# Second attention: exponentials mixed in single precision as the moving operand, values in 32-column groups

## The reference, cut to what matters

```python
    def _L1_attn_ref(hidden_states, W_attn, b_attn, P_q, P_k, P_v, W_back, W_proj, b_proj):
        B, S, D, DC, H = (4, 512, 192, 96, 12)
        HD = DC // H
        b, s, _ = hidden_states.shape
        qkv = hidden_states @ W_attn + b_attn
        q, k, v = jnp.split(qkv, 3, axis=-1)
        q = q @ P_q
        k = k @ P_k
        v = v @ P_v
        split = lambda t: t.reshape(b, s, H, HD).transpose(0, 2, 1, 3)
        qh, kh, vh = (split(q), split(k), split(v))
        scores = jnp.einsum('bhqd,bhkd->bhqk', qh, kh) / jnp.sqrt(jnp.float32(HD))
        causal = jnp.tril(jnp.ones((s, s), dtype=scores.dtype))
        scores = scores * causal + -10000.0 * (1.0 - causal)
        weights = jax.nn.softmax(scores, axis=-1)
        ctx = jnp.einsum('bhqk,bhkd->bhqd', weights, vh)
        ctx = ctx.transpose(0, 2, 1, 3).reshape(b, s, DC)
        out = ctx @ W_back
        out = out @ W_proj + b_proj
        return out
```

## Time and profile before

| | |
|---|---|
| median of the runs | 991.69 us |
| the runs | 990.14, 994.79, 991.69 us |
| profiled execution, from first to last instruction | 992.2 us |
| granted TensorE clock, mean of the span | 0.787 |
| TensorE matmuls busy | 726.5 us (73%) |
| VectorE busy | 696.7 us (70%) |
| ScalarE busy | 672.9 us (68%) |
| GpSimd busy | 345.5 us (35%) |

### The profile page before, as it was taken

How to read it: one execution, slowest core, us unless ns; L and a number is a source line. 1 busy time by engine, 2 the same in 40 slices (tenths; PEclk the granted TensorE clock), 3 DMA queues, 4 the chain that set the end, 5 groups by cost and what they waited for, 6 DMA issues and landing times. The chain is left out here.

```text
span 992.2 us, 19112 instructions
## 1 busy us (share of the span) xinstructions
PE 726.5 (73%) x7022; PEld 534.0 (54%) x7023; DVE 696.7 (70%) x1406; ACT 672.9 (68%) x1236; POOL 345.5 (35%) x265
## 2 busy tenths in 40 slices
PE   2693661452696748999997488867775898999985
PEld 1562330221475424599997444324444467999984
DVE  3588989999598888654453476986988874554543
ACT  1578947999697858755554279568993761767664
POOL 6720920000000000468775424680000202577763
PEclk9786555555698757999999789555557899999999
DMA  6446770000221319534333466370002952243332
GB/s 190 137 84 190 210 219 10 8 17 0 72 79 57 130 52 327 170 46 60 60 52 50 97 258 227 135 289 35 3 1 81 343 208 72 42 60 56 56 45 33
DMA packets 61397, 105.71 MB, mean 107 GB/s; under 512 B 9705, under 2 KB 43196, under 8 KB 61068
## 3 DMA queue, kind: packets, MB, share of 16 engines
q1 hardware_dynamic: 44940, 88.21, 26.9%
q0 software_dynamic: 16384, 16.53, 10.9%
HBM read 76.84 MB, written 27.87 MB: 106 GB/s over the span
## 5 line engine op out<-in xcount | busy, mean ns | idle before, releaser
L2383 DVE COPY m_xgT<-m_px 128x768 f16<-128x768 f16 (+1 forms) x46 | 22.9, 497 | 120.3 <-PE m_px L2228 116.3
L2350 ACT ACTIVATE m_pu<-m_pu,m_b,m_unit 128x256 f32<-128x256 f32 (+1 forms) x138 | 63.7, 509 | 57.4 <-PE m_pu L2260 55.9
L2391 DVE SCALAR_TENSOR_TENSOR m_hT<-m_pu,m_unit,m_hT 128x512 f16<-128x512 f32 (+1 forms) x138 | 85.8, 663 | 17.5 <-ACT m_hT L2343 17.4
L1140 ACT ACTIVATE a_ex<-m_pieces,a_nb 128x256 bf16<-128x256 f16 x192 | 94.3, 494 | 5.4 <-DVE a_nb L1166 5.4
L977 PE MATMUL a_pp<-a_room 16*128 16x256 bf16 x240 | 55.9, 412 | 41.6 <-DVE m_pieces L1154 31.8
L2354 ACT ACTIVATE m_pu<-m_pu,m_unit 128x512 f32<-128x512 f32 (+1 forms) x69 | 41.1, 596 | 65.1 <-PE m_pu L2260 65.1
L2343 ACT ACTIVATE m_hT<-m_pu,m_unit 128x512 f16<-128x512 f32 (+1 forms) x138 | 81.5, 635 | 0.0
L2194 POOL DMA_INDIRECT m_xg<-xn_d,m_token x70 | 69.8, 997 | 30.7 <-issue 20.6
L2202 POOL DMA_INDIRECT out_h<-m_yo,m_token x39 | 62.1, 1592 | 39.4 <-DVE m_yo L2401 27.9
L2202 POOL DMA_INDIRECT h_d<-m_yo,m_token x39 | 62.0, 1591 | 38.0 <-DVE m_yo L2401 21.4
L2260 PE MATMUL m_pu<-m_xgT,m_w 128*128 128x256 f16 (+1 forms) x690 | 69.7, 260 | 1.3 <-DVE m_xgT L2383 1.3
(11 more groups left out here) (495 smaller groups left out, 1877.6 us busy)
## 6 DMA issues: line engine op xcount, KB each, us to landing
m_pieces<-in_m_w SPq DMA_DIRECT2D x11, 768.0 KB, 5.3
a_early_w<-in_m_w SPq DMA_DIRECT2D x10, 768.0 KB, 5.4
hv_raw<-in_m_w SPq DMA_DIRECT2D x8, 768.0 KB, 5.8
w1h_d<-hv_parts SPq DMA_DIRECT2D x8, 768.0 KB, 4.1
m_w<-w1h_d SPq DMA_DIRECT2D x8, 768.0 KB, 9.1
m_pieces<-in_m_w SPq DMA_DIRECT2D x8, 576.0 KB, 6.1
a_room<-in_m_w SPq DMA_DIRECT2D x8, 576.0 KB, 3.7
hv_raw<-in_m_w SPq DMA_DIRECT2D x8, 576.0 KB, 5.5
```

The source lines that it names most:

```text
L1140: last = act.activation(ex[:, n % 2, r], v16t[:, n, r, :], ACT.Exp, bias=nbt[:, n, r:r + 1], scale=scale, accum_out=sumst[:, n, r:r + 1])
L2350: act.activation(pu[:, u, n, q * w:(q + 1) * w], pu[:, u, n, q * w:(q + 1) * w], ACT.Relu, bias=b1[:, bass.ds(e * FC + 2 * n + q, 1)], sca ...
L2391: last = v.scalar_tensor_tensor(hT[:, u, 1, third], pu[:, u, n, 0:2 * w], unit[:, 1:2], hT[:, u, 0, third], ALU.mult, ALU.subtract)
```

## The change

The exponentials stay in single precision and are no longer split. They become the moving operand, and the values the stationary one, in single precision, 32 columns per head. `vv` holds for each token tile three runs of 128 + 9 columns, so that the 32 columns taken for head h hold its 8 values and a one at offset 9 times (h // 4), and zeros otherwise. The sums of the heads with equal h modulo 4 then fall into the same 32 partitions of the accumulator, 9 rows each. Once per image VectorE copies the sums out (`flat`), TensorE turns them with two transposes, and VectorE inverts and multiplies. The whole of `vv` is zeroed by GpSimd ahead of the projection, and the values are put in place by three activations per turn. The cuts of the values into bfloat16 parts are gone. The scale of the exponential is read from a register.

```diff
-    VW = PARTS * HD1 + 1
+    VW = HD1 + 1
+    COLS = 4 * 32
...
-        vv = c.sb("a1_vv", [P, NT, H, HD1], F32, s)
-        vp = c.sb("a1_vp", [P, NT, H, VW], BF16, s)
+        vv = c.sb("a1_vv", [P, NT, GROUPS * (COLS + VW)], F32, s)
...
+        def columns_of(t, h):
+
+            first = h // 4 * COLS + h % 4 * 32
+            return vv[:, t, first:first + 32]
+
+        def own(t0, t1, d0, d1):
+
+            return vv[:, t0:t1, :].rearrange("p t (u x) -> p t u x", u=GROUPS)[:, :, :, 0:COLS]\
+                .rearrange("p t u (j x) -> p t u j x", j=4)[:, :, :, :, d0:d1]
...
-                        pool.memset(vp[:, :, :, VW - 1:VW], 1.0).then_inc(cleared, 1)
+                        pool.memset(vv[:], 0.0).then_inc(cleared, 1)
                         pool.wait_ge(cleared, 3)
+                        for u in range(GROUPS):
+                            pool.memset(own(0, NT, HD1, VW)[:, :, u], 1.0).then_inc(cleared, 1)
+                        pool.wait_ge(cleared, 3 + GROUPS)
...
-                                    act.activation(vv[:, 4 * i:4 * i + 4],
-                                                   pq[:, n % 4, 0:4 * DK].rearrange("p (t h d) -> p t h d", t=4, h=H),
-                                                   ACT.Identity, scale=vscale).then_inc(vkept, 1)
+                                    act.wait_ge(cleared, 3)
+                                    src = pq[:, n % 4, 0:4 * DK].rearrange("p (t u j d) -> p t u j d", t=4, u=GROUPS, j=4)
+                                    for u in range(GROUPS):
+                                        last = act.activation(own(4 * i, 4 * i + 4, 0, HD1)[:, :, u], src[:, :, u],
+                                                              ACT.Identity, scale=vscale)
+                                    last.then_inc(vkept, 1)
...
-                                if n - Halves.FRONT < PARTS:
-                                    cast_v(n - Halves.FRONT)
...
-                                if 0 < n - Halves.FRONT + 1 < PARTS:
-                                    less_v(n - Halves.FRONT)
...
-                        def mix(i, n):
...
-                                        for r in range(2):
-                                            last = nc.tensor.matmul(
-                                                pc[:, n // 2 % 2, first:first + VW],
-                                                hl[:, n % 4, r, hh, blk * P:(blk + 1) * P],
-                                                vnow[:, n // 4, kt, h, :],
-                                                start=(kt == 0 and r == 0), stop=(kt == qt and r == 1))
-                            last.then_inc(mixed[n % 4], 1)
...
+                        def mix(n):
+
+                            img = n // UNITS
+                            pe.wait_ge(raised[n % 2], n // 2 + 1)
+                            if n % UNITS == 0 and img >= 2:
+                                pe.wait_ge(taken, 2 * (img - 1))
+                            for kt in range(2):
+                                for hh in range(HG):
+                                    h = HG * (n % UNITS) + hh
+                                    r0 = 32 * (h % 4)
+                                    last = nc.tensor.matmul(pc[r0:r0 + 32, img % 2, 0, kt * P:S],
+                                                            columns_of(2 * img + kt, h),
+                                                            e[:, n % 4, hh, 2 * kt * P:(2 + kt) * P],
+                                                            start=(kt == 0 and h < 4), stop=(kt == 1 and h >= H - 4))
+                            last.then_inc(mixed, 1)
+
+                        def turn_context(img):
+                            pe.wait_ge(copied, img + 1)
+                            for t in range(2):
+                                last = nc.tensor.transpose(pc[:, img % 2, 1, t * P:(t + 1) * P],
+                                                           flat[:, img % 2, t * P:(t + 1) * P], c.ident[:])
+                            last.then_inc(turned, 1)
+
+                        score(0)
+                        score(1)
+                        for n in range(UNITS * B):
+                            if n + 2 < UNITS * B:
+                                score(n + 2)
+                            mix(n)
+                            if n % UNITS == 0 and n > 0:
+                                turn_context(n // UNITS - 1)
+                        turn_context(B - 1)
...
-                                if n % 4:
-                                    act.wait_ge(raised[j], i * 4 + n // 2 + 1)
-                                    act.wait_ge(mixed[n % 4], i * 2 + n // 4)
-                                    act.activation(hl[:, n % 4, 0], e[:, n % 4], ACT.Copy, scale=LIFT)\
-                                       .then_inc(high[1], 1)
...
+                        for n in range(UNITS * B):
+                            act.wait_ge(scored, n + 1)
+                            if n >= 4:
+                                act.wait_ge(mixed, n - 3)
+                            act.activation(e[:, n % 4], pb[:, n % 2, :, 0:3 * P], ACT.Exp, scale=scale)\
+                               .then_inc(raised[n % 2], 1)
...
+                        for img in range(B):
+                            j = img % 2
+                            dve.wait_ge(mixed, UNITS * (img + 1))
+                            v.tensor_copy(flat[:, j, :], pc[:, j, 0, :]).then_inc(copied, 1)
+                            dve.wait_ge(turned, img + 1)
...
+                            for t in range(2):
+                                last = v.reciprocal(inv[:, j, t], rows_of[:, t, :, :, HD1])
+                            last.then_inc(inverted, 1)
+                            dve.wait_ge(inverted, img + 1)
+                            for t in range(2):
+                                v.tensor_tensor(cx[:, 2 * img + t].rearrange("p (u j) d -> p j u d", j=4),
+                                                rows_of[:, t, :, :, 0:HD1],
+                                                inv[:, j, t].unsqueeze(3).to_broadcast([P, 4, GROUPS, HD1]),
+                                                ALU.mult).then_inc(taken, 1)
```

More of the change, by code:

```diff
@@ L3241, in turn @@
-                        def turn(i, ahead):
-                            for n in range(8):
-                                if n + 2 < ahead:
-                                    score(i, n + 2)
-                                if n >= 1:
-                                    mix(i, n - 1)
-                                elif i >= 1:
-                                    mix(i - 1, 7)
-                        score(0, 0)
-                        score(0, 1)
-                        for i in range(turns - 1):
-                            turn(i, 10)
@@ L3272, in _ @@
-                        turn(0)
-                        for i in range(1, turns):
-                            turn(i)
+                        scale = act.alloc_register("a1_scale")
+                        act.reg_load(scale, sscale[0:1, :].bitcast(I32))
+                        for n in range(UNITS * B):
[4 more added lines that the diff above has]
+                               .then_inc(raised[n % 2], 1)
@@ L3311, in turn @@
-                        def turn(i):
-                            for img in range(2):
-                                v.tensor_copy(vnow[:, img], vp[:, bass.ds(i * 4 + 2 * img, 2), :, :])\
-                                 .then_inc(copied, 1)
-                            for n in range(8):
-                                if n % 4 == 0:
-                                    split_high(i, n)
-                                split_low(i, n)
-                                if n % 2 == 1 and n > 2:
-                                    take(i, n // 2 - 1)
-                            take(i, 3)
@@ L3323, in _ @@
-                        turn(0)
-                        for i in range(1, turns):
-                            turn(i)
-                        dve.wait_ge(taken[0], 2 * turns)
-                        dve.wait_ge(taken[1], 2 * turns)
+                        for img in range(B):
[3 more added lines that the diff above has]
+                            dve.wait_ge(turned, img + 1)
+                            rows_of = pc[:, j, 1, :].rearrange("p (t j x) -> p t j x", t=2, j=4)[:, :, :, 0:GROUPS * VW]\
+                                .rearrange("p t j (u d) -> p t j u d", u=GROUPS)
+                            for t in range(2):
[7 more added lines that the diff above has]
+                                                ALU.mult).then_inc(taken, 1)
```

90 lines of the change are left out of this document (17 added, 73 removed).

## The result

The changed kernel takes **977.13 us** (median of 4 runs, 973.21 to 980.29), the kernel before on the same chip 991.88 (4 runs, 990.14 to 994.79): a ratio of 0.984, with a 95% interval of 0.981 to 0.987. That is faster by 14.8 us. The forecast was 986.5 with a range of 969 to 1016. The profiled execution spans 978.3 us, 13.9 less than that of before.

A forecast was written before the change was run, and what follows sets the result against it. No engine alone bounded the mixing block: ScalarE, VectorE and TensorE stood within ten microseconds. Terms -2.6 - 1.5 + 1.2 - 2.3 = -5.2 us took the 992.2 span to 987.0, median 986.5; own range 979 to 993, 8-in-10 range 969 to 1016.

The forecast's parts named there:

- block: Mixing block: with 1.90 us units on TensorE it ends at 743.7 and not 746.3, 2.6 us less.
- output transposes: Output block: its transposes, entered at the full clock, take half the time, 1.5 us less.
- projection: Projection: three activations placing values instead of one cost 1.2 us more; GpSimd's zeroing costs nothing.
- maxima block: Maxima block: without the casts and GpSimd's two subtractions the splitting starts earlier, 2.3 us less, between 0 and 2.3.
- The unit on TensorE: Mixing block: score 0.26, mask 0.32, mixing 1.12 with heads overlapping two at a time, tile changes 0.20: 1.90 us.
- The rival that overlaps all three: Mixing block: all three heads' column groups overlap, mixing 0.64 us, unit 1.42, total 971 us; chance 0.12.
- The estimate from the Trainium skill's 2.38 times: Mixing block: three column tiles at 2.38 times one give a mixing of 0.81 us, not adopted.
- The serial rival: Mixing block: column groups do not overlap in single precision, unit 2.70 us, total 1012 us; chance 0.19.
- The clock: Mixing block: full clock after two units at 1.2 GHz; the rival staying at 1.2 GHz gave 1037 us, chance 0.11.
- The weight loads: Mixing block: taken as hidden; the rival where they show, 0.146 us each, gave 1068 us, chance 0.05.
- Turns and tail: Mixing block: seven turns of an image's sums at 0.3 us each, and 2.0 us uncovered behind the last mixing.

The follow-up runs named there:

- the run with everything moved apart: Changed kernel with zeroes in four placed pieces and GpSimd's first two halves of weights held back until VectorE's third and fourth subtraction groups ended: 972.03 us, ratio 0.980.

## Why the prediction was right and wrong

The sign and the range held; the size did not: 14.8 us came where 5.2 were forecast. The time lies below the forecast's own range of 979 to 993, and within the wide one only because that reached to the rivals. By its own terms, forecast against measured: block -2.6 against -17.5, output transposes -1.5 against -0.8, projection +1.2 against +5.2, maxima block -2.3 against -3.6.

**The unit on TensorE.** Score with its change of tiles was put at 0.26 and is 0.27; the mask with its change at 0.42 and is 0.43. The step that failed is "matmuls keep their order, and the second record of a head must follow its first in the same columns, so only that second record and the next head's first can run together". The first half does not hold across column groups: the first records of all three heads start within 14 ns, ahead of the second record of any. So the mixing streams in 0.65 us (two records of 256 and two of 128 columns, at the starts shown above), the lower bound that the prediction had worked out as 0.64, and with the change of tiles it is 0.78 where 1.12 and 0.10 stood. That is 0.42 us too much in the unit, 13 of the 15 us by which the block was missed. The rest is the start: units of 2.62 and 2.03 us (678.13 to 680.16, in the middle of which the clock rose) where two of 3.5 were allowed. The rival that overlaps all three, at 1.42 us a unit, was the true one, and it had 0.12. Its "against", that two records of one head share their columns, speaks only against six at a time. The estimate from the Trainium skill's 2.38 times, some 10 us less than forecast, was nearer than the forecast, in part by luck, as the projection's further loss of 4 us was in neither.

**The serial rival** was priced well: unit 2.70, and one column group gave 2.77; 1012 us, and it gave 1019.

**The clock** went as taken. The granted clock was 0.50 in the maxima block and rose while the first single precision products of 128 rows and 32 columns ran, and all but the start of the second mixing runs at full speed. In the changed kernel and the twelve experiments it rose 2.4 to 5.4 us after the first of these products, with one column group (3.7 us) as with three. At 1.2 GHz a unit would be 2.62, by this trace 32 times 1.14 or 36 us more, an estimate by which the change would lose. What made it rise was not tried by itself.

**The weight loads** are hidden, all 384: the full mixing is no longer than its streaming and one change of tiles. A load took 0.111 us here, where the rival's price used 0.146. The Trainium skill's sentence ("TensorE: Matmul & The Clock Gate", Part 3) that loads overlap only where row groups differ does not hold here, as the earlier trace rows had already said.

**Turns and tail.** A turn takes 0.37 (703.58 to 703.95) where 0.3 was put, the copy 0.425 where 0.4.

**The projection.** Three activations for one were put at 0.4 us a turn and three turns; in the first turn they take 0.88 us for 0.60, but the run with everything moved apart has 55.72 against 55.96 before, so this term is nothing that shows. The other term, "GpSimd stands idle for 12.85 us before its first half of weights, and the old memset goes: nothing", failed, and cost 5.2. Cover was asked of GpSimd's own queue only. The memset took 5.58 us, not 8.8, and was indeed over in time for its successor. What was not asked is who else runs beside it: VectorE's scalings and additions with a number per partition (TENSOR_SCALAR), in single precision from SBUF to SBUF, stand still while GpSimd works. The Trainium skill ("SBUF — State Buffer", "SBUF: two separate sides") says that VectorE's two-port operations and GpSimd share a pair of ports as an exclusive lock, that the one that starts first has it for its whole instruction, and that the other blocks. The trace agrees: 6.32 us against 1.25, 4.53 against 0.17. Over the second attention in all fourteen traces, 37 such instructions of 4 or 192 numbers started while a memset or a subtraction of GpSimd still had more than their own time to run, and all 37 were held. Of the statistics and reciprocals, which are single precision from SBUF to SBUF too, none of 167 was, and operations from PSUM stood only behind a held one. By that rule the new memset would have been a price of up to its length on the first normalisation. The kernel before already showed it: 1.48 us for its first group, beside a memset of 0.97, against 1.25 for the others, and, plainer, 1.24 us for the addition ahead of that group against 0.17.

**The maxima block.** The splitting starts 26.1 us after the first maximum (650.02 less 623.89), as worked out. Yet the hole shrank by 1.1 and not 2.3: the step "they wait for TensorE, which waits for ScalarE's copy, behind GpSimd's splitting" left out that the transposes also need a bank whose maxima VectorE has taken, and at 655.26 it is this that they wait for. Two gains were not foreseen, against the step "Nothing else of the casts lies on the path". The scaling of 72 numbers meets GpSimd's subtraction for a shorter time (1.85 to 0.71 us): in both kernels it ends 0.05 us behind it. And ScalarE loads its table at 666.48, ahead of its wait, where before the load stood behind it (1.28 us). 1.1, 1.1 and 1.3 are 3.5 of the 3.6. The lines of the kernel before:

```profile
667.02 1.85 DVE L3063 TENSOR_SCALAR a_neg<-a_neg 128x72 f32<-128x72 f32 x1
672.13 1.28 ACT L3098 ACT_TABLE_LOAD   x1 [5.75 <-DVE a_rows L3169]
```

**The output transposes** start at 728.11 at the full clock and take 1.92, but the products behind them then wait for VectorE: 0.8 of 1.5 us came.

What stays open: the stages behind the block took 241.3 us in the profiled execution of the changed kernel and 237.3 in that of before. In the twelve experiments, with the same code there, they took 236.9 to 242.3, so this is not laid to the change; what sets it was not looked for.

## What to carry to other kernels

Small products that are put into different column groups of TensorE run side by side, in single precision too, and a unit's twelve records took as long in either order of the loops: bound such a group by its slowest column group, and take that bound as the forecast unless a row speaks against it.

A new GpSimd instruction has two prices: its successor in its own queue, and every single precision scaling or addition of VectorE from SBUF to SBUF beside it, which can stand for its whole length (statistics, reciprocals and what reads PSUM were not held here). List what VectorE runs in that stretch before writing "nothing", and remember that moving GpSimd's work moves the collision; here only keeping the two apart removed it.

When an engine becomes the sole bound, look at what the freed ones can take from it: here the mask, 5.4 us (54.38 to 48.94).

## What was unexpected of the hardware

Column groups behave as if each had a queue of its own: starts 6 to 14 ns apart, and 0.43 us out of program order.

GpSimd holds an addition on 4 numbers for 4.53 us as it holds four subtractions of 192, and a memset of one partition holds an operation on all 128 (1.24 us for 0.17). Pieces back to back let some operations in and not others.

GpSimd's first subtraction comes 6.74 to 6.96 us after its last memset where its input is ready earlier (four runs), and the waits show nothing for it but "issue". The Trainium skill ("GPSIMD Engine Reference", "Instruction dispatch") says that the first call of a freshly loaded routine pays about 6 us, with no instruction to be seen; that would fit, and was not tried by itself. If it is so, it would be why delaying a memset also delayed the weights.

An exponential of 1152 numbers takes 1.13 us with its scale in a register and 1.22 with the scale from a tile.
